# Context columns of two groups loaded behind the first quarter of x, later weights behind the opening

## The reference

```python
x = x + _L0_xattn_ref(_layernorm(x), ctx, ctx, pad, Wq, bq, Wk, bk, Wv, bv, Wo, bo, 1)  # 16 heads of 8, causal
x = x + _L0_ffn_ref(_layernorm(x), Wr, br, W1, b1, W2, b2)          # 16 experts, top 2, gelu
x = x + _L1_xattn_ref(_layernorm(x), ctx, mask, Wq, Wkv, Wo)        # 2 heads of 64
x = x + _L1_ffn_ref(_layernorm(x), up, gate, down, router, ...)     # 8 experts, top 1, silu, and a shared one
```

## Time and profile before

| | us |
|---|---|
| median of three runs (lowest, highest) | 1006.11 (1004.85, 1008.36) |
| the profiled execution, its own time | 1005.86 |
| its span | 1004.0 |
| TensorE busy | 821.1 (82%) |
| VectorE busy | 666.0 (66%) |
| ScalarE busy | 578.2 (58%) |
| GpSimd busy | 511.1 (51%) |

### The profile page before, as it was taken

The page is one execution under the profiler, slowest core; times in us unless marked ns, Lnnn a source line. Parts: engine busy times, 40 slices in busy tenths (PEclk is TensorE's granted clock), DMA queues, the critical chain, the costliest instruction groups (busy, mean ns, idle before and its releaser), DMA issues. The chain is left out here.

```text
span 1004.0 us, 27974 instructions
## 1 busy us (share of the span) xinstructions
PE 821.1 (82%) x9234; PEld 689.1 (69%) x9234; DVE 666.0 (66%) x2294; ACT 578.2 (58%) x1339; POOL 511.1 (51%) x612
## 2 busy tenths in 40 slices
PE   0699999999999820999998178888858998959997
PEld 0478877878777710999997055555547887849996
DVE  3788899999989742344446379999963546425554
ACT  0588888888888500666665177777756551213332
POOL 4011145555564765344445677777400644726777
PEclk9799999999999855999999599999998999979999
DMA  6000011111116413344332233333213213244441
GB/s 206 11 19 18 14 39 37 47 44 40 49 40 194 143 45 101 112 135 136 131 125 94 72 83 78 82 82 79 55 31 124 85 67 118 107 137 141 145 122 55
DMA packets 67572, 86.33 MB, mean 86 GB/s; under 512 B 22000, under 2 KB 50037, under 8 KB 66960
## 3 DMA queue, kind: packets, MB, share of 16 engines
q1 hardware_dynamic: 47728, 44.71, 15.2%
q0 software_dynamic: 17152, 39.36, 12.1%
q10 hardware_dynamic: 2592, 0.95, 0.5%
HBM read 50.47 MB, written 35.01 MB: 85 GB/s over the span
## 5 line engine op out<-in xcount | busy, mean ns | idle before, releaser
L1155 POOL DMA_INDIRECT f_rows_in<-f_xn_all,f_pos_i x128 | 126.1, 985 | 68.5 <-DVE a_mx L389 34.4
L758 POOL DMA_INDIRECT a_got<-f_rows_out,f_pos_i x128 | 122.7, 958 | 41.5 <-issue 35.4
L1155 POOL DMA_INDIRECT f_rows_in<-f1r_xn_all,f_pos_i x64 | 61.6, 962 | 70.8 <-DVEq L1222 31.3
L1552 POOL DMA_INDIRECT out<-f1e_y,f1e_ids x72 | 76.5, 1062 | 41.3 <-DVE f1e_y L1611 24.7
L1560 POOL DMA_DIRECT2D f_rows_out<-f0e_y x80 | 43.8, 547 | 88.3 <-DVE f0e_y L1614 71.4
L1664 ACT ACTIVATE f0e_hT<-f0e_ps_h,f0e_w 128x256 f32<-128x256 f32 (+1 forms) x160 | 63.8, 449 | 38.5 <-PE f0e_ps_h L1694 38.5
L1614 DVE TENSOR_TENSOR f0e_y<-f0e_ps_y,f0e_w 128x256 f32<-128x256 f32 (+1 forms) x80 | 31.7, 397 | 80.9 <-PE f0e_ps_y L1704 80.6
L618 PE MATMUL a_ps_o<-vx,a_prT 128*64 128x18 f32 x2048 | 83.6, 215 | 2.0 <-DVE x_sb L419 2.0
L618 PEld LDWEIGHTS a_ps_o<-vx,a_prT 128*64 128x64 f32 x2048 | 79.7, 140 | 7.7 <-issue 4.7
L293 POOL TENSOR_TENSOR x_sb<-x_sb,bo 128x256 f32<-128x256 f32 x32 | 23.3, 727 | 116.3 <-DVE a_xn L354 116.0
L389 DVE TENSOR_REDUCE a_mx<-a_ps_s 128x16 f32<-128x1024 f32 x64 | 77.7, 1215 | 5.1 <-PE a_ps_s L589 4.9
(11 more groups left out here) (300 smaller groups left out, 2043.3 us busy)
## 6 DMA issues: line engine op xcount, KB each, us to landing
f1e_x<-f_rows_in SPq DMA_DIRECT2D x32, 272.0 KB, 2.7
a_ctxT<-in_ctxT SPq DMA_DIRECT2D x64, 128.0 KB, 2.1
f0e_x<-f_rows_in SPq DMA_DIRECT2D x64, 128.0 KB, 2.0
f_rows_out<-f0e_y POOLq DMA_DIRECT2D x64, 128.0 KB, 2.0
f_w<-in_f_w SPq DMA_DIRECT2D x16, 257.0 KB
x_sb<-in_x SPq DMA_DIRECT2D x4, 1024.0 KB, 5.0
f_w<-in_f_w SPq DMA_DIRECT2D x8, 384.0 KB, 6.4
f_rows_in<-f_xn_all,f_pos_i POOLq DMA_INDIRECT x128
```

The lines of the kernel that those rows point to most:

```text
L758: pool.indirect_dma_start(got[:, n, k, :], None, N.rows_out[0:N.most, :], bass.IndirectOffsetOnAxis(ap=N.pos_i[:, k, t:t + 1], axis=0)).th ...
L1155: pool.indirect_dma_start(N.rows_in, bass.IndirectOffsetOnAxis(ap=N.pos_i[:, k, t:t + 1], axis=0), self.xn_all[:, t, :], None).then_inc(se ...
L1552: pool.indirect_dma_start(rows_of_out, bass.IndirectOffsetOnAxis(ap=ids[:, n, u:u + 1], axis=0), y[:, n, u, :], None, bounds_check=B * S - ...
```

## The change

Three things. The tile `ctxT` moves from the attention block to the tiles that live through the kernel, so that it can be filled from the opening. SP issues the context loads of groups 0 and 1 in the opening, between the first quarter of x and the wait for `w_loaded`, each with a semaphore of its own (`ctx_first`), and TensorE's first projections wait for those; the other waits count one filling less. The eight DMAs of `later` go from the end of SP's opening to the head of its attention block, ahead of the context load of group 2.

```diff
--- before.py
+++ after.py
@@ -71,7 +71,7 @@
         R.x_loaded = [sem(f"x{c}") for c in range(X_CHUNKS)]
         w_loaded, made, own_ready, st_done = sem("w_loaded"), sem("made"), sem("own_ready"), sem("st_done")
         spread_ready, bias_done, sharp_made = sem("spread_ready"), sem("bias_done"), sem("sharp_made")
-        R.later_loaded = sem("later_loaded")
+        R.later_loaded, R.ctx_first = sem("later_loaded"), [sem(f"ctx{g}") for g in range(2)]
         bvs = ctx.enter_context(nc.sbuf_tensor("op_bvs", [P, P], F32))
         warm = ctx.enter_context(nc.sbuf_tensor("op_warm", [P, 1], F32))
         ps_b = ctx.enter_context(nc.psum_tensor("op_ps_b", [P, 512], F32))
@@ -83,6 +83,7 @@
         later = [(R.w1[n][:, :], A["a1_" + n]) for n in ("wq", "wk", "wv", "wo")]
         for tag, (wr, br) in R.router.items():
             later += [(wr[:, :], A[tag + "_wr"]), (br[:, :], A[tag + "_br"].partition_broadcast(P))]
+        R.later_loads = later
         R.later = len(later)
 
         @block.sync
@@ -90,10 +91,10 @@
             for c in range(X_CHUNKS):
                 tiles = slice(c * n, (c + 1) * n)
                 if c == 1:
+                    for g in range(2):
+                        sp.dma_start(R.ctxT[:, g, :], A["ctxT"][:, GT * g:GT * (g + 1)]).then_inc(R.ctx_first[g], 16)
                     sp.wait_ge(w_loaded, 16 * len(first))
                 sp.dma_start(R.x[:, tiles, :], R.xd[:, tiles, :]).then_inc(R.x_loaded[c], 16)
-            for place, data in later:
-                sp.dma_start(place, data).then_inc(R.later_loaded, 16)
 
         @block.scalar
         def _(act):
@@ -228,7 +229,7 @@
         ps = lambda name, shape: ctx.enter_context(nc.psum_tensor("a0_" + name, shape, F32))
         sem = lambda name: R.semaphore(nc, "a0_" + name)
         x_sb, ident, w = R.x, R.ident, R.w0
-        ctxT = sb("ctxT", [P, 2, GT])
+        ctxT = R.ctxT
         xn, xnT = sb("xn", [P, 2, C]), sb("xnT", [P, GT])
         qx, kx = sb("qx", [P, 2, GT]), sb("kx", [P, 2, PER, GT])
         vx = R.vx0
@@ -278,7 +279,11 @@
             def body(i):
                 for g in range(2):
                     load(2 * i + g, g)
-            rounds(sp, body, NG // 2, last=0)
+            for place, data in R.later_loads:
+                sp.dma_start(place, data).then_inc(R.later_loaded, 16)
+            body(1)
+            with sp.Fori(2, NG // 2) as i:
+                body(i)
             K.load_weights(sp, shared=False)
             sp.wait_ge(R.later_loaded, 16 * R.later)
             sp.wait_ge(zeros_made, 1)
@@ -554,7 +559,10 @@
         @block.tensor
         def _(pe):
             def proj_xk(G, g, use):
-                pe.wait_ge(loaded[g], 16 * (use + 1))
+                if use == 0:
+                    pe.wait_ge(R.ctx_first[g], 16)
+                else:
+                    pe.wait_ge(loaded[g], 16 * use)
                 pe.wait_ge(xn_ready, 2 * G + 2)
                 if needed(G):
                     pe.wait_ge(qv_ready, G)
@@ -1735,6 +1743,7 @@
 
         self.own, self.own_bk = sb("own", [P, PER]), sb("own_bk", [P, PER])
         self.vx0 = sb("vx0", [P, 2, 4, PAIRS, 2, D0 + 1])
+        self.ctxT = sb("ctxT", [P, 2, GT])
         self.kx1 = sb("kx1", [P, 2, H1, GT])
         self.vx1 = sb("vx1", [P, 4, 4, P + H1])
         self.xd = A["x"]
```

## The result

| | before | after |
|---|---|---|
| median of 15 timed runs each (lowest to highest), us | 1005.67 (1004.03 to 1012.46) | 1000.89 (996.2 to 1003.51) |
| mean of the same runs | 1006.9 | 1000.2 |
| the profiled execution: span | 1004.0 | 999.9 |
| VectorE's first maximum in it | 38.05 | 29.98 |

The ratio is 0.9933, with a 95% interval of 0.9914 to 0.9952: 6.7 us faster, between 4.8 and 8.6. The means differ by 6.7 us, the medians by 4.8 only, because the runs of before fall into two groups, nine at 1004.0 to 1006.1 and six at 1008.0 to 1012.5, and the median lies in the lower one. A second comparison (9 runs against 26) gave 0.9944, 0.9926 to 0.9963. Forecast were 7.3 us less and 998.8 in all; the measured median is 2.1 us above that and lies in the range.

The account below looks back on a forecast made before the run. The prediction took a slackless chain from TensorE's late first projection, then a full attention loop, as the bound. Terms -7.9 + 0.3 + 0.3 = -7.3 us from 1005.86, plus 0.25 for the median, gave 998.8; range 996.2 to 1002.8.

Parts of the forecast that it names:

- The barrier, 4.0 us earlier: Between opening and attention block: without SP's eight later loads VectorE comes last, and the barrier falls 4.0 us earlier.
- The context wait, 3.9 more: TensorE's first projection: waits for norm(0) instead of the context columns, starting at about 15.2, 3.9 us gained.
- norm(1) meets GpSimd, +0.3: VectorE's second normalization pair, at 16.8, runs beside GpSimd's kx clear and loses 0.3 us.
- Context in front of the weights, +0.3: Opening: two context DMAs (262 KB) before w_loaded take 0.6 us at 420 GB/s, half hidden, costing 0.3 us.
- Later loads ahead of group 2's context; x; moved tile: SP's later issues are covered by group 2's wait, x has 3.6 us slack, ctxT's new address costs nothing.
- What the first projection gains, the end gains: From the first projection on, chain and attention loop have no slack, so its whole gain reaches the end.
- Its own sign: First maximum at 30.7 instead of 38.05, with the same shift, within 2 us, at attention's end and span's end.
- 1.5 us each way: Range allowance for where the TensorE clock rises again; nothing for it in the sum.
- Rival A: Behind the barrier norm(0) goes before GpSimd's vx clear, taking 0.60 not 1.93 us: -8.6 us, 997.5; chance 0.14.
- B: First projection, under full DMA load, starts only as x ends, at 20.3: 2.8 us gained, 1003.3; chance 0.09.
- C: Something else holds the loop, such as GpSimd's start-up or the statistics' end: no change, 1006.1; chance 0.05.
- D: TensorE's clock stays at 1.2 GHz through the first passes; 20 further low us give +2.7, 1008.8; chance 0.04.

Follow-up runs that it names:

- e1: Changed kernel with the context loads back at the head of the attention block, so only the later loads moved; ratio to before 0.9993.
- e2: Changed kernel with the eight later loads back at the end of SP's opening, so only the context loads moved; ratio to before 0.9962.
- e5: Changed kernel plus eight further context loads (1.05 MB) into an unread tile, ahead of the w_loaded wait; profiled once, not timed, copy of bv at 13.27 us.
- e4b: Changed kernel with the 48 statistics taken a second time behind the first; median 1009.75 us, ratio to before 1.0023.
- first and third execution: Two of three profiled executions of the unaltered changed kernel; leads over before's first trace at 37 and 997 us: 8.06 and 4.07, 8.43 and 5.60.
- e3: Changed kernel with GpSimd's first clear (vx) held back until norm(0) is done; median 998.25 us of 4 runs, ratio to before 0.9914.
- e9d: Changed kernel with statistics four a pass in passes 0 to 11, deviations by Ln and Exp on ScalarE, clear behind norm(0); median 1010.41 us, ratio 1.0038.

## Why the prediction was right or wrong, step by step

- *The barrier, 4.0 us earlier.* Right: all go on at 12.9 instead of 17.1. SP came last in before, VectorE does now. e1 shows this half alone.
- *The context wait, 3.9 more.* Right: the first projection starts at 15.09 against 15.2, released by norm(0), as forecast. e1 and e2 show that each half uncovers the other.
- *norm(1) meets GpSimd, +0.3.* Too much: it took 0.68 instead of 0.60. It starts at 16.64, 0.2 us before the kx clear ends, and nothing of it reached the statistics, which start 2.06 us behind the first projection (2.10 in before).
- *Context in front of the weights, +0.3.* Too much: nothing that can be told from the spread of 10.5 to 11.2 between traces. But the reason given, that half of it hides in holes of the DMA engines, does not carry: in e5 1.05 MB more found 2.7 us of holes and cost 2.3 us. So this term came out small without its reason being shown.
- These two terms, and weights that came 0.2 earlier than in the trace of before (10.93, 11.14), are why the front gained 8.06 and not 7.3.
- *Later loads ahead of group 2's context; x; moved tile.* Right: SP waits until 21.29, the statistics take 9.37 us without a gap, and the lead is constant over the loop.
- *What the first projection gains, the end gains.* Right until 325 us, and e4b still pays 8.8 of its 9.4 us at 250. It failed at the phases' edges, where TensorE idles and its clock falls: steps of 0.3 to 2.7 us. Its own sign, the same shift within 2 us at the end of the span, failed in the first and third execution (8.06 and 4.07, 8.43 and 5.60) and held in the second (8.25 and 6.88). The sum should have had a term there, and "1.5 us each way" was too small: two profiled executions of one kernel differ by 2.8 (changed) and 1.4 (before) at the end, and the 15 timed runs of each kernel lie 7.3 and 8.4 us apart.
- *Rival A* (VectorE first behind the barrier) did not happen, but e3 shows its size: 1.33 us. *B and C* did not happen: TensorE starts at 15.09, 0.15 us behind norm(0), in a DMA share of 1.00. *D* happened in part and elsewhere: from 37 us on an execution lost 1.4 to 4.0 us in all, beside stretches at the low clock that were longer or further ones, not 7.3, and mostly not in the first passes.

That the total came out near the forecast is in part luck: a front 0.8 us better than forecast and a loss at the clock that was not in the sum cancel each other in part.

## What to carry to other kernels

Ask of every barrier who comes last, and of every first wait what is late next: two waits in a row hide each other, and taking both is worth more than the sum of each alone. A small load in front of others can be free (262 KB here), but do not reckon by the idle share of the DMA engines how much more would be: 1.05 MB found room by that share and still held up the weights by 2.3 us. Measure it at the wait that stands behind them. In a loop that is full for one engine, work moved into it must be free on its own engine and also not stand in front of anything another engine waits for; look at the instruction behind it in its queue, not at the engine's busy share.

## What the runs showed of the hardware

- VectorE's pair of normalizations takes 1.93 us where it starts with GpSimd's memset of 128x2080 (1.84 us), in every trace here, and 0.60 us where it goes ahead of it; the memset takes 1.84 us either way. The bn_stats are not slowed beside GpSimd's additions: 48 take 9.37 us in the changed kernel, beside 1.41 us of them, and 9.38 in the second set of e4b, with GpSimd idle.
- A table load on ScalarE takes 1.28 us and the next activation mostly starts 1.29 to 1.30 us behind the load's start. Ln and Exp each reloaded the table in e9d, whose loop also uses Exp: three times two loads.
- The first rows of a profile print a granted clock of 1.00 where there is no record, though the matmuls there have the durations of 1.2 GHz (16 of them in 1.12 us, as at a printed 0.50).
- A us at 1.2 instead of 2.4 GHz in the first passes costs 0.45 to 0.55 us; a TensorE gap of 3 us in the loop (e9d) costs 5.4 us together with the clock that follows.
